# A Mamba and channel-mix layer: the start laid out anew, with channel mix's weights on GpSimd's queue and other orders of the steps

## The chip, the core and the metric

The kernel runs on one core of a Trainium2 chip. Its five engines work side by side and wait for each other by semaphores: PE (TensorE, matrix products into PSUM), DVE (VectorE), ACT (ScalarE), POOL (GpSimd) and SP, which here only issues transfers. A transfer can be issued from the queue of SP, of ACT or of POOL. The metric is the time of one execution on the device in microseconds (us); shorter is better. PSUM has eight banks of 128 x 512 f32: here two hold the sum y (y_ps), three the decays (da_ps), and three (w0_ps, w1_ps, w2_ps) are shared by all other products.

## What is computed

x is 4 x 2048 x 256, f32. Two blocks follow each other, each added to its input:

```python
# Mamba block on xn = layernorm(x)
xz = xn @ W_in;  x_, z = halves of xz;  proj = x_ @ W_x
delta = softplus(proj[..., :D] @ W_dt + b_dt);  B, C = the 2*16 other columns of proj
h = exp(delta * A[n]) * h + delta * x_ * B[n]        # along the sequence, for 16 states n
y = sum over n of h * C[n] + x_ * D_param
h1 = x + layernorm((y * silu(z)) @ W_out + xn) * ln_g + ln_b
# channel mix on hn = layernorm(h1), hp = hn of the token before
r = sigmoid((mu_r*hn + (1-mu_r)*hp) @ W_r.T)
k = relu((mu_k*hn + (1-mu_k)*hp) @ W_k.T)**2
out = h1 + r * (k @ W_v.T)
```

## The kernel before

**Tiling.** The tokens are cut into 16 chunks of 512 (4 per sequence). Step t works at once on three or four chunks: it scans chunk t, prepares chunk t+1 (the units xnT, bc, dt, x, z), finishes the Mamba block of chunk t-1 (gT, wo, xa) and does channel mix for chunk t-2 (hT, r, k, v, xo). Step -1 is the start, with the preparation of chunk 0 alone; step 15 and `close` are the end.

**A step.** The scan of a chunk has 16 columns (states n). For each, ACT makes the decays exp(delta*A) of both channel halves in da_ps (L646); POOL makes dbx = u * B (L530, up to three columns ahead of the step's own count, in a ring of four); DVE scans both halves (L1018). Times C and into hg: on DVE for the columns in `SPLITS` (L1025), on POOL for the others (L543). PE adds hg into y_ps by products with the identity (L1267). The carry of a column to the next chunk is copied by ACT (L652, L657). With three da_ps banks, ACT can be at most about one column and a half ahead of DVE.

**What sets the order.** All other work is hung between these columns by hand-written tables: `ACT_TURN` and `VEC_TURN` name a place (0 to 31, two for each column), `PE_TURN` a column (0 to 15), `BANK` one of the three shared banks. `_HEAD` and `_TAIL` tables do the same for step -1 and step 15. Each engine runs its list strictly in order, so a stage that waits holds up all that stands behind it on its engine.

**The start.** SP loads W_in, W_x, x, W_dt and then nine further things: mu_r, mu_k, ln_b, W_r, W_k, W_v, W_out, ln_g, ln_b again, all counted on one semaphore (`w_loaded`, 9 loads). PE turns W_in by transposes (`turn_weight`, L1218), multiplies W_x and then W_dt into it (L1229, L1236), and ACT copies each result out of PSUM (`folded_weight`, L620), so that delta comes from xn in one product. DVE takes the moments of x (L953), ACT its rsqrt (`first_rsqrt`), DVE the norm (L967); PE turns xn (L1301), ACT copies it to xnT. Then PE makes bc (the B and C rows), dt, x, z. bc goes through HBM and comes back spread over all partitions (b_ring, c_ring); only the first two B rows are spread on the chip, by products with `pick` (L1346) that ACT copies to b_ring (L694, `first_column`).

After these, at place 25 of its list, DVE scales channel mix's weights (`scale_ffn_weights`, L976 to L983): PE turns W_r, W_k (in the banks of the two spread rows, so it waits for both copies, `b_begun`) and then W_v (`turn_ffn_weights`, at column 12), and DVE writes six results. Then DVE takes the norm of chunk 1. All of it stands ahead of the first scan in DVE's list. One semaphore, `start_read`, counts how many of the start's units are read, in their order.

## Time and profile before

| | us |
|---|---|
| median of 3 runs | 975.38 (974.22 to 981.02) |
| the profiled execution, whole | 975.23 |
| its span on the core | 973.4 |

| engine | busy us | share of the span | instructions |
|---|---|---|---|
| PE | 897.7 | 92% | 4830 |
| DVE | 906.3 | 93% | 921 |
| ACT | 851.6 | 87% | 2060 |
| POOL | 885.5 | 91% | 392 |

The span is what lies between the first and the last instruction on the core; the time of a run is 1.8 us longer here. Every row of a timeline gives the start, how long the engine was busy, the engine, the line of the code, what was written from what, how many instructions are merged, and in brackets how long the engine had been idle and what ended that. A run of n instructions that overlap a little takes less than n times the duration of one.

### The profile page before, as it was taken

To read this page: it belongs to the slowest core of one execution; us is meant where nothing else is said; L and a number is where in the kernel's file an instruction comes from. 1 tells how busy PE (TensorE), PEld (TensorE's weight loads), DVE (VectorE), ACT (ScalarE), POOL (GpSimd) and SP (SyncE) were. 2 spreads that over 40 slices of the span, in tenths; PEclk is the share of its full clock that TensorE was granted. 3 is DMA by queue.
4 is the path that set the end of the run, shared out by engine and by line. 5 is a ranking of instruction groups with operands and counts; after the bars stand their busy time and mean duration, and the time that the engine had idled before them with its cause. 6 is when DMAs were issued, how large, how long until landed. Compare 5 with 4: busy or idle time off the path is not lost.

```text
span 973.4 us, 15457 instructions
## 1 busy us (share of the span) xinstructions
PE 897.7 (92%) x4830; PEld 695.1 (71%) x4830; DVE 906.3 (93%) x921; ACT 851.6 (87%) x2060; POOL 885.5 (91%) x392
## 2 busy tenths in 40 slices
PE   7676787999999999999999999999999999999997
PEld 4345475777877677786777688776868778788886
DVE  2799999999999999999999999999999999999765
ACT  3486888999999999998999999999999999988855
POOL 1689999999999989999999989999999998999970
PEclk9798787999999999999999999999999999999999
DMA  6426553465455626355454635556353644544320
GB/s 192 169 89 216 198 199 127 152 238 177 174 219 195 231 101 248 139 197 197 195 196 160 252 113 200 193 196 240 150 196 133 238 165 184 215 174 156 130 76 23
DMA packets 51472, 171.44 MB, mean 176 GB/s; under 512 B 5440, under 2 KB 32576, under 8 KB 35136
## 3 DMA queue, kind: packets, MB, share of 16 engines
q1 hardware_dynamic: 50576, 170.44, 47.8%
q8 instruction: 39, 0.64, 0.3%
q14 instruction: 41, 0.34, 0.1%
q10 hardware_dynamic: 816, 0.02, 0.0%
HBM read 153.15 MB, written 9.44 MB: 167 GB/s over the span
## 4 chain that ended last, share of the span: by engine, by line
PE 51%; ACT 26%; DVE 16%; issue 7%; DMA 0%; DVEq 0%; ACTq 0%
PE w_ps L1276 13%; PE w_ps L1283 10%; PE y_ps L1267 8%; ACT da_ps L646 8%; DVE da_ps L1018 6%; PE w_ps L1292 5%; PE w_ps L1295 5%; DVE hg L1018 4%; ACT h_tok L596 3%; DVE hg L1025 3%; PE w_ps L1360 3%; PE w_ps L1301 3%; ACT xres L850 2%; ACT h_tok L582 2%; ACT xn_tok L582 2%
## 5 line engine op out<-in xcount | busy, mean ns | idle before, releaser
L530 POOL TENSOR_TENSOR dbx<-u,b_ring 128x1024 f32<-128x1024 f32 x255 | 599.3, 2382 | 14.9 <-DVE da_ps L1018 6.4
L646 ACT ACTIVATE da_ps<-delta,a_neg 128x512 f32<-128x512 f32 x512 | 343.1, 685 | 17.4 <-DVE hg L1025 10.6
L543 POOL TENSOR_TENSOR hg<-hg,c_ring 128x1024 f32<-128x1024 f32 x123 | 292.5, 2378 | 18.1 <-ACT carry L652 17.9
L1267 PEld LDWEIGHTS y_ps<-ident,hg 128*128 128x128 f32 x2048 | 233.8, 143 | 43.9 <-issue 28.7
L1267 PE MATMUL y_ps<-ident,hg 128*128 128x128 f32 x2048 | 255.1, 276 | 10.3 <-POOL hg L543 10.3
L1018 DVE TENSOR_TENSOR_SCAN da_ps<-da_ps,carry,dbx 128x512 f32<-128x512 f32 x200 | 245.7, 1272 | 2.5 <-ACT da_ps L646 2.5
L1018 DVE TENSOR_TENSOR_SCAN hg<-da_ps,carry,dbx 128x512 f32<-128x512 f32 x184 | 224.9, 1267 | 5.8 <-ACT da_ps L646 5.4
L1025 DVE TENSOR_TENSOR hg<-da_ps,c_ring 128x1024 f32<-128x1024 f32 x132 | 160.9, 1219 | 8.4
L1018 DVE TENSOR_TENSOR_SCAN da_ps<-da_ps,dbx 128x512 f32<-128x512 f32 x64 | 75.5, 1215 | 1.9 <-ACT da_ps L646 1.7
L1018 DVE TENSOR_TENSOR_SCAN hg<-da_ps,dbx 128x512 f32<-128x512 f32 x64 | 75.3, 1210 | 2.1 <-ACT da_ps L646 1.9
L1276 PE MATMUL w_ps<-xnT,w_in 128*128 128x512 f32 x120 | 58.3, 631 | 4.8 <-DVE zs L1054 4.5
L1292 PE MATMUL w_ps<-w_rT,mixed 128*128 128x256 f32 x240 | 61.7, 380 | 1.0 <-DVE mixed L1062 1.0
L1295 PE MATMUL w_ps<-w_r_prev,mixed 128*128 128x256 f32 x240 | 61.6, 379 | 0.0
L1283 PE MATMUL w_ps<-w_in,xnT 128*128 128x256 f32 x248 | 59.6, 384 | 0.2 <-ACT delta L680 0.2
L1276 PE MATMUL w_ps<-mixed,w_kT 128*128 128x512 f32 x120 | 57.0, 598 | 2.6 <-DVE mixed L1062 2.6
L1283 PE MATMUL w_ps<-w_out,gated 128*128 128x256 f32 x248 | 58.6, 379 | 0.0
L1276 PE MATMUL w_ps<-xnT,w_dtx 128*128 128x512 f32 x120 | 55.0, 601 | 1.3 <-DVE mixed L1062 0.7
L1283 PE MATMUL w_ps<-w_vT,kact 128*128 128x256 f32 x240 | 54.4, 379 | 0.0
L1283 PEld LDWEIGHTS w_ps<-w_out,gated 128*128 128x128 f32 x248 | 47.1, 190 | 6.4
L1295 PEld LDWEIGHTS w_ps<-w_r_prev,mixed 128*128 128x128 f32 x240 | 45.6, 190 | 6.2
L1283 PEld LDWEIGHTS w_ps<-w_in,xnT 128*128 128x128 f32 x248 | 45.6, 193 | 5.7 <-ACT delta L680 0.5
L1292 PEld LDWEIGHTS w_ps<-w_rT,mixed 128*128 128x128 f32 x240 | 44.3, 190 | 7.0 <-DVE mixed L1062 1.2
(194 smaller groups left out, 1339.4 us busy)
## 6 DMA issues: line engine op xcount, KB each, us to landing
c_ring<-bc_rows_dram SPq DMA_DIRECT2D x64, 1024.0 KB, 4.7
b_ring<-bc_rows_dram SPq DMA_DIRECT2D x63, 1024.0 KB, 6.3
xres<-in_L_attn_x_in_dram SPq DMA_DIRECT2D x16, 512.0 KB, 4.8
x_tok<-in_L_attn_x_in_dram SPq DMA_DIRECT2D x15, 512.0 KB, 5.9
res<-xn_tok SPq DMA_DIRECT2D x15, 512.0 KB, 3.2
out_dram<-r_out SPq DMA_DIRECT2D x15, 512.0 KB, 3.2
bc_rows_dram<-bc_rows SPq DMA_DIRECT2D x16, 64.0 KB, 6.4
w_in<-in_L_attn_W_in_dram SPq DMA_DIRECT2D x2, 256.0 KB, 4.5
```

The source lines that it names most:

```text
L530: pool.tensor_tensor(dbx[:, n % X_RING, :, :], u[:, ip, :, :], b.to_broadcast([P, KH, LC]), ALU.mult).then_inc(s["dbx_done"], 1)
L543: pool.tensor_tensor(part, part, c_of(n).to_broadcast([P, KH, LC]), ALU.mult).then_inc(s["g_pool"], 1)
L582: last = act.activation(dst[j], src[j], ACT.Identity, scale=rs[j], bias=nm[j])
L596: last = act.activation(spare[:, j, :], src[:, j, :], ACT.Square, bias=nm[ln][:, j:j + 1], accum_out=sq[ln][:, j:j + 1])
L646: act.activation(da_of(n, h), delta[:, ip, h, :], ACT.Exp, scale=a_neg[:, h, n:n + 1]).then_inc(s["da_ready"], 1)
L1018: dve.tensor_tensor_scan(out, da_of(n, h), dbx[:, n % X_RING, h, :], 0.0 if first else carry[:, n, h:h + 1], ALU.mult, ALU.add).then_inc(s ...
L1025: dve.tensor_tensor(hg[:, n % H_RING, :, :], da_both(n), c_of(n).to_broadcast([P, KH, LC]), ALU.mult).then_inc(s["g_vec"], 1)
L1267: last = pe.matmul(y_tok[:, b, h * P:(h + 1) * P], hg[:, n % H_RING, h, b * P:(b + 1) * P], ident[:, :], is_transpose=True, start=n == 0 a ...
L1276: last = pe.matmul(out, w[:, k, cols], x[:, k, :], start=k == 0, stop=k == KH - 1)
L1283: last = pe.matmul(by_block(out)[:, b, :], xT_[:, k, tokens], w[:, k, :], start=b == 0 and k == 0 and not begun, stop=k == KH - 1, skip_gr ...
L1292: pe.matmul(by_block(out)[:, b, :], h_of[:, k, at_b + 1:at_b + 1 + P], w_rT[:, k, :], start=k == 0, stop=False)
L1295: last = pe.matmul(by_block(out)[:, b, :], h_of[:, k, at_b:at_b + P], w_r_prev[:, k, :], start=False, stop=k == KH - 1)
```

## The change

1. **Transfers.** W_r, W_k, mu_r, mu_k, W_v, W_out, ln_g, ln_b (twice) are issued from POOL's queue, after the identity and `pick`, and no more from SP's. `w_loaded` (now four loads) is split: `w_r_in`, `w_kv_in`, `mu_loaded` stand for the others.
2. **The start in places of its own.** `scale_ffn_weights` and `turn_ffn_weights` are cut into three, and `first_column`, `softplus`, `scale_x`, `first_rsqrt(1)`, `first_norm(1)` each get a place. On PE, W_r and W_k are turned ahead of bc, W_v after the spread rows; on ACT the moments' rsqrt comes ahead of the copy of wxT; on DVE the three scalings are spread. `start_read` becomes six semaphores, so that the units can be read in any order.
3. **Products of zeros.** DVE writes zeros to kact; PE multiplies them twice (128 x 512) ahead of everything else.
4. **Tables.** All of `ACT_`, `VEC_`, `PE_` `TURN`, `HEAD`, `TAIL`, `BANK` and `TAIL_BANK` have other numbers. The work is the same.

```diff
-ACT_HEAD = dict(xnT0=17, bc=19, xnT1=19, sp=25)
-VEC_HEAD = dict(small=5, second=7, u0=16, u1=22, ffn=25)
+ACT_HEAD = dict(xnT0=1, xnT1=3, bc=3, sp0=3, sp1=9, x1=16, rsq1=24, col0=25, x0=26, col1=30)
+VEC_HEAD = dict(ffn0=2, second=3, small=11, u1=13, ffn1=14, u0=16, norm=26, ffn2=31)
...
-            for dst, src in loads:
-                sp.dma_start(dst, src).then_inc(s["w_loaded"], 16)
...
+            pool.dma_start(raw[0], halves(W_r)).then_inc(s["w_r_in"], 16)
+            pool.dma_start(raw[1], halves(W_k)).then_inc(s["w_kv_in"], 16)
+            for dst, v in ((mur, mu_r), (muk, mu_k)):
+                pool.dma_start(dst[:, :], column(v), allow_slow_non_contiguous=True).then_inc(s["mu_loaded"], 16)
+            pool.dma_start(raw[2], halves(W_v)).then_inc(s["w_kv_in"], 16)
+            pool.dma_start(w_out[:, :, :], halves(W_out)).then_inc(s["w_loaded"], 16)
...
                         folded_weight(0, w_inT, by_half(work[0]))
-                        folded_weight(1, wxT, by_half(work[1]))
                         act.wait_ge(s["a_loaded"], 48)
...
                         first_rsqrt(0)
+                        folded_weight(1, wxT, by_half(work[1]))
...
+            dve.memset(kact[:, 0, :], 0.0).then_inc(s["warm_set"], 1)
...
+            pe.wait_ge(s["warm_set"], 1)
+            for _ in range(2):
+                pe.matmul(work[1][:, :], kact[:, 0, 0:P], kact[:, 0, :], start=True, stop=True)
...
+            def turn_ffn_weight(m):
+                if m == 0:
+                    pe.wait_ge(s["w_r_in"], 16)
+                else:
+                    pe.wait_ge(s["w_kv_in"], 32)
+                if m < 2:
+                    pe.wait_ge(s["setup_ev"], 2 + m)
+                else:
+                    pe.wait_ge(s["b_begun"], 1)
+                turn_weight(FFN_BANKS[m], raw[m]).then_inc(s["ffn_turned"], 1)
...
                 def first_column(m):
...
+                    pe.wait_ge(s["pick_set"], HEAD_COLS)
+                    need_read(pe, t, "bc")
+                    pe.wait_ge(s["setup_ev"], 4)
+                    pe.wait_ge(s["ffn_set"], m + 1)
```

**DVE's list from the first norm to the first scans, before** (`w_in<-w_in` halves W_z; `w_r_prev` to `w_vT` are the scaled weights; the second `xn_tok` is the norm of chunk 1; a scan prints as SCALAR_TENSOR_TENSOR):

```order
L962 TENSOR_SCALAR w_in<-w_in 128x2x256
L988 TENSOR_SCALAR a_neg<-gated 128x32
L953 BN_STATS gated<-x_tok 128x6 x4
L957 BN_AGGR gated<-gated 128x2 x4
L1046 TENSOR_TENSOR u<-da_ps,delta 128x512
L1046 TENSOR_TENSOR u<-y_ps,delta 128x512
L976 TENSOR_SCALAR omr<-mur 128x2
...
L983 TENSOR_SCALAR w_kT<-w_ps 128x512
L983 TENSOR_SCALAR w_vT<-w_ps 128x512
L967 TENSOR_SCALAR xn_tok<-x_tok,gated,rs 128x256 x4
L1018 SCALAR_TENSOR_TENSOR da_ps<-da_ps,dbx 128x512 x2
```

The same stretch of the change:

```order
L973 TENSOR_SCALAR w_in<-w_in 128x2x256
L987 TENSOR_SCALAR omr<-mur 128x2
...
L994 TENSOR_SCALAR w_rT<-w_ps,mur 128x256
L964 BN_STATS gated<-x_tok 128x6 x4
L968 BN_AGGR gated<-gated 128x2 x4
L1001 TENSOR_SCALAR a_neg<-gated 128x32
L1059 TENSOR_TENSOR u<-da_ps,delta 128x512
L996 TENSOR_SCALAR w_kT<-w_ps 128x512
L1059 TENSOR_TENSOR u<-y_ps,delta 128x512
L978 TENSOR_SCALAR xn_tok<-x_tok,gated,rs 128x256 x4
L996 TENSOR_SCALAR w_vT<-w_ps 128x512
L1031 SCALAR_TENSOR_TENSOR da_ps<-da_ps,dbx 128x512 x2
```

W_r's four results went ahead of the second moments, W_k's between the two u; of the scalings only W_v's is left behind the norm of chunk 1.

**PE's list at the start, before** (`w_ps<-ident,h_tok` and `<-ident,gated_tok` turn W_r, W_k and W_v; `xnT,w_bc` is bc, `xnT,w_dtx` dt, `xnT,w_in` x; `w_in,xnT` is z; `bc_rows,pick` spreads a B row; the row `w_in,ident` only keeps PE busy):

```order
L1276 MATMUL w2_ps<-xnT,w_bc 32x512 x2
L1276 MATMUL da_ps<-xnT,w_dtx 128x512 x2
L1276 MATMUL da_ps<-xnT,w_in 128x512 x2
L1346 MATMUL w1_ps<-bc_rows,pick 128x512
L1276 MATMUL da_ps<-xnT,w_dtx 128x512 x2
L1276 MATMUL y_ps<-xnT,w_in 128x512 x2
L1346 MATMUL w0_ps<-bc_rows,pick 128x512
L1218 MATMUL w0_ps<-ident,h_tok 128x128 x4
L1218 MATMUL w1_ps<-ident,h_tok 128x128 x4
L1218 MATMUL w0_ps<-ident,gated_tok 128x128 x4
L1283 MATMUL y_ps<-w_in,xnT 128x256 x4
```

and of the change:

```order
L1232 MATMUL w1_ps<-ident,h_tok 128x128 x4
L1232 MATMUL w0_ps<-ident,h_tok 128x128 x4
L1295 MATMUL w2_ps<-xnT,w_bc 32x512 x2
L1295 MATMUL da_ps<-xnT,w_dtx 128x512 x4
L1295 MATMUL da_ps<-xnT,w_in 128x512 x2
L1295 MATMUL y_ps<-xnT,w_in 128x512 x2
L1362 MATMUL w0_ps<-bc_rows,pick 128x512
L1362 MATMUL w1_ps<-bc_rows,pick 128x512
L1232 MATMUL w1_ps<-ident,gated_tok 128x128 x4
L1302 MATMUL y_ps<-w_in,xnT 128x256 x4
```

Both turns of W_r and W_k now stand ahead of bc, and both spread rows behind dt and x.

**PE's list in a middle step, before** (from column 4; `ident,gated_tok` is gT, `w_rT,mixed` and `w_r_prev,mixed` are r, `ident,hg` adds a column to y):

```order
L1283 MATMUL w0_ps<-w_in,xnT 128x256 x4
L1267 MATMUL y_ps<-ident,hg 128x128 x8
L1283 MATMUL w1_ps<-w_in,xnT 128x256 x4
L1301 MATMUL w2_ps<-ident,gated_tok 128x128 x4
L1267 MATMUL y_ps<-ident,hg 128x128 x8
L1292 MATMUL w0_ps<-w_rT,mixed 128x256 x2
...
L1301 MATMUL w1_ps<-ident,gated_tok 128x128 x4
L1267 MATMUL y_ps<-ident,hg 128x128 x8
L1276 MATMUL w1_ps<-xnT,w_in 128x512 x2
L1276 MATMUL w0_ps<-xnT,w_in 128x512 x2
```

and of the change:

```order
L1320 MATMUL w1_ps<-ident,gated_tok 128x128 x4
L1302 MATMUL w0_ps<-w_in,xnT 128x256 x4
L1302 MATMUL w2_ps<-w_in,xnT 128x256 x4
L1320 MATMUL w1_ps<-ident,gated_tok 128x128 x4
L1286 MATMUL y_ps<-ident,hg 128x128 x8
L1295 MATMUL w0_ps<-xnT,w_in 128x512 x2
L1286 MATMUL y_ps<-ident,hg 128x128 x8
L1311 MATMUL w1_ps<-w_rT,mixed 128x256 x2
...
L1286 MATMUL y_ps<-ident,hg 128x128 x8
L1295 MATMUL w0_ps<-xnT,w_in 128x512 x2
```

Both gT and the first x (`xnT,w_in`) now stand ahead of r, and u0, which DVE makes from that x, moved from place 20 to 16.

## Rows read from the trace of the kernel before

**Rows 1.** The page: its head and busy time by engine.
```profile
span 973.4 us, 15457 instructions
PE 897.7 (92%) x4830; PEld 695.1 (71%) x4830; DVE 906.3 (93%) x921; ACT 851.6 (87%) x2060; POOL 885.5 (91%) x392
```

**Rows 2.** Windows: steps 0, 8, 9 and 15, each from its first scan.
```profile
core 0: us, PE busy (x) PEld busy (x) DVE busy (x) ACT busy (x) POOL busy (x), PEclk, DMA share, GB/s
35.64:91.44 55.80, 39.93 (x174) 26.75 (x172) 52.58 (x54) 38.12 (x82) 45.50 (x20) 0.83 0.41 147
486.55:541.96 55.41, 53.91 (x302) 42.46 (x301) 53.72 (x55) 53.14 (x134) 54.35 (x24) 1.00 0.53 191
541.96:598.67 56.71, 54.44 (x302) 42.40 (x301) 56.12 (x56) 53.96 (x137) 53.53 (x24) 1.00 0.51 187
879.47:943.61 64.14, 62.82 (x373) 53.28 (x372) 52.69 (x51) 50.09 (x105) 62.20 (x28) 1.00 0.33 119
```

**Rows 3.** The same view, from POOL's first product with C that follows a wait.
```profile
57.05:205.30 148.25, 120.11 (x626) 91.79 (x625) 142.40 (x135) 126.52 (x314) 145.09 (x63) 0.87 0.50 183
```

**Rows 4.** The chain that ended last, at the start: start us, us, what.
```profile
15.25 1.90 PE w_ps L1276 x4
...
20.79 1.05 PE w_ps L1346 x2
...
28.35 1.66 DVE omr L976
...
33.59 2.12 DVE xn_tok L967 x4
```

**Rows 5.** Timeline of DVE, at the start.
```profile
8.06 0.38 DVE L957 BATCH_NORM_AGGREGATE gated<-gated 128x2 f32<-128x6 f32 x4
...
35.64 2.33 DVE L1018 TENSOR_TENSOR_SCAN da_ps<-da_ps,dbx 128x512 f32<-128x512 f32 x2
...
45.12 2.32 DVE L1001 TENSOR_SCALAR w_out<-w_out,gated 128x256 f32<-128x256 f32 x2
```

**Rows 6.** Timeline of PE, at the start.
```profile
4.50 1.09 PE L1218 MATMUL w_ps<-ident,w_in 128*128 128x128 f32 x4 [4.50 <-DMA w_in<-in_L_attn_W_in_dram]
6.33 3.78 PE L1229 MATMUL w_ps<-c_ring 128*128 128x256 f32 x8 [0.75 <-ACT c_ring L620]
10.80 1.99 PE L1236 MATMUL w_ps<-c_ring 128*128 128x256 f32 x8 [0.69 <-ACT c_ring L620]
```

**Rows 7.** Timeline of ACT, at the start.
```profile
21.88 0.60 ACT L694 ACTIVATE b_ring<-w_ps 128x512 f32<-128x512 f32 x1 [2.08 <-PE w_ps L1346]
...
27.43 1.91 ACT L646 ACTIVATE da_ps<-delta,a_neg 128x512 f32<-128x512 f32 x3
```

**Rows 8.** The page's queues: transfer, issues, KB each, us from issue to landing.
```profile
h_tok<-in_L_ffn_W_r_dram SPq DMA_DIRECT2D x1, 256.0 KB, 4.1
```

**Rows 9.** Timeline of POOL: the first products, and those around step 1.
```profile
22.56 1.27 POOL L522 TENSOR_TENSOR dbx<-u,b_ring 128x512 f32<-128x512 f32 x1 [20.07 <-ACT b_ring L694]
...
27.63 6.97 POOL L530 TENSOR_TENSOR dbx<-u,b_ring 128x1024 f32<-128x1024 f32 x3
...
44.69 2.34 POOL L543 TENSOR_TENSOR hg<-hg,c_ring 128x1024 f32<-128x1024 f32 x1 [0.62 <-ACT carry L652]
...
94.77 4.69 POOL L530 TENSOR_TENSOR dbx<-u,b_ring 128x1024 f32<-128x1024 f32 x2
```

**Rows 10.** Timeline of DVE: third column of step 1, then the waits of step 8.
```profile
97.49 2.44 DVE L1018 TENSOR_TENSOR_SCAN da_ps<-da_ps,carry,dbx 128x512 f32<-128x512 f32 x2
...
522.00 0.69 DVE L1046 TENSOR_TENSOR u<-w_ps,delta 128x512 f32<-128x512 f32 x1 [0.31 <-PE w_ps L1276]
...
524.06 1.23 DVE L1018 TENSOR_TENSOR_SCAN da_ps<-da_ps,dbx 128x512 f32<-128x512 f32 x1 [0.23 <-ACT da_ps L646]
...
539.64 1.22 DVE L1018 TENSOR_TENSOR_SCAN hg<-da_ps,dbx 128x512 f32<-128x512 f32 x1 [0.53 <-ACT da_ps L646]
```

**Rows 11.** Timeline of PE in step 8: the last products of r.
```profile
517.76 1.03 PE L1295 MATMUL w_ps<-w_r_prev,mixed 128*128 128x256 f32 x4
```

More of the change, by code:

```diff
@@ L303, in need_bank @@
             if at_start(t):
-                need(eng, s["start_read"], max([use_of(t, unit) - len(START_BANKS)] + [use_of(t, v) for v in after]))
+                turn = HEAD_UNITS.index(unit)
+                before = [HEAD_UNITS[turn - len(START_BANKS)]] if turn >= len(START_BANKS) else []
+                for v in before + list(after):
+                    need_read(eng, t, v)
             else:
@@ L412, in _ @@
             sp.dma_start(w_in[:, :, D:], halves(W_in)[:, :, D:]).then_inc(s["w_z_loaded"], 16)
-            loads = [(raw[0], halves(W_r)), (raw[1], halves(W_k)), (raw[2], halves(W_v)), (w_out[:, :, :], halves(W_out))]
-            loads += [(dst[:, :], v.rearrange("(o d) -> o d", o=1).partition_broadcast(P))
-                      for dst, v in ((g_all, ln_g), (b_all, ln_b))]
-            for dst, v in ((mur, mu_r), (muk, mu_k), (b_col, ln_b)):
-                sp.dma_start(dst[:, :], column(v), allow_slow_non_contiguous=True).then_inc(s["w_loaded"], 16)
-            for dst, src in loads:
-                sp.dma_start(dst, src).then_inc(s["w_loaded"], 16)
             def slot_before(i, g):
@@ L1087, in step @@
                         first_moments(1)
-                    if start and at("ffn"):
-                        scale_ffn_weights()
+                    for m in range(3):
+                        if start and at(f"ffn{m}"):
+                            scale_ffn_weight(m)
+                    if start and at("norm"):
                         first_norm(1)
@@ L1426, in step @@
                                           is_transpose=True, start=False, stop=False, skip_group_check=True)
-                    if start and n == turn["ffn"]:
-                        turn_ffn_weights()
+                    for m in range(3):
+                        if start and n == turn[f"ffn{m}"]:
+                            turn_ffn_weight(m)
+                    for m in range(2):
+                        if start and n == turn[f"col{m}"]:
+                            first_column(m)
                     behind = column_at(t, par, n - Y_LAG, scan, pre, mid)
```

143 lines of the change are left out of this document (68 added, 75 removed).

## The prediction

> **What bounds the kernel now.** I read the page first: over the whole span four engines are busy 87% to 93% of the time [rows 1], so no share says which one sets the pace. Cutting the span at the first scan of each step does. In a middle step DVE is busy 53.72 of 55.41 us or 56.12 of 56.71 [rows 2]: its idle time is 1.7 us in step 8 and 0.6 in step 9, and part of the 0.6 is the short turn between a scan and the product that reads it. PE, ACT and POOL have 1 to 3 us left in the same steps. So DVE sets the middle steps, the others are close behind, and an order that is better can give back about 1 us in a step like 8, of which there are three (4, 8 and 12, whose sequence starts anew), and next to nothing elsewhere.
>
> The two ends differ. DVE's first scan starts at 35.64 [rows 5]. In step 0 DVE is idle for only 3.2 of 55.8 us; POOL is idle for 10.3 there [rows 2], but from 57.05 to 205.30 it works 145.09 of 148.25 us [rows 3]. In that stretch it is at least as tight as DVE: the product for the third column of step 1 is the first of the two that run from 94.77 for 4.69 us, so it is over at about 97.1 [rows 9], and the scan that reads it starts at 97.49 [rows 10]. So in steps 0 to 2 a faster DVE alone would soon wait for POOL, and only a shift that takes POOL along comes through. In step 15 PE is busy 62.82 of 64.14 us [rows 2]: the end hangs on PE, whose work does not change.
>
> The start is where the time lies. In the chain that ended last, bc's product starts at 15.25 and the spread row ends at 21.84 (20.79 + 1.05); then the scalings of channel mix's weights start at 28.35 and the norm of chunk 1 at 33.59, which lasts 2.12 us [rows 4]. From 28.35 to the scan at 35.64, 7.3 us, DVE does nothing that the first scan needs, while decays are there from 27.43 on [rows 7] and POOL has its ring full at 34.60 (27.63 + 6.97) [rows 9].
>
> **The change, part by part.** I lay the new start out with these durations.
>
> *Zeros, and the chain to bc.* Today PE is idle until W_in lands, and turns it at 4.50. The eight products with W_x take 3.78 us, while eight of the same form take 1.99 us from 10.80 on [rows 6]: TensorE is at the lower of its two clocks (1.2 GHz) before and at the upper (2.4) after. The zeros are two 128 x 512 products; four rows of that form, two products, take 1.90 us at the upper clock [rows 4], so some 3.8 at the lower. PE is free from about 1.5 us, so they end at about 5.2: the turn of W_in starts 0.7 later. If the clock rises by the time of the W_x products, these give back up to 3.78 - 1.99 = 1.8. Bounds: +0.7 (no earlier rise) to -1.1. But ACT now takes the rsqrt of x's moments ahead of the copy of wxT. The moments are done at 8.44 [rows 5] if x lands as now, and W_r and W_k will share the transfers of x and W_dt; I allow them 0.5 us. That leaves a gain of 0.9 of the 1.1. Then PE turns W_r and W_k ahead of bc: four transposes take 1.09 at the lower clock [rows 6], so two turns take 1.1 at the upper, of which some 0.7 lie in the gap in which PE waits for xnT anyway. bc starts at 15.25 - 0.9 + 0.4 = 14.75.
>
> *From bc to the first scan.* Three units (bc, dt, x) fill 15.25 to 20.79, 1.85 each [rows 4]. Now five stand ahead of the spread rows: 14.75 + 9.2 = 23.95. Two spread rows at 1.05: 26.0. ACT's copy 0.6 [rows 7], its copy of x 0.6 more, and the first decay a third of 1.91, 0.65 [rows 7]: 27.9. Meanwhile DVE has u1, W_k's scaling, u0 and the norm of chunk 1 (no more behind POOL's products, see below) done by about 26; W_v is turned after the first copy (26.6 + 0.55) and scaled by about 27.8. **First scan at 27.9 instead of 35.64: 7.8 us.** POOL's first product moves the other way, from 22.56 [rows 9] to 26.6, and it then has no wait for u. Can POOL take that up? From 22.56 to step 1 at 91.44 are 68.9 us, of which it is idle for 2.6 (23.83 to 26.4, between the two halves of its first column [rows 9]) and 10.3 [rows 2]: 56.0 of work. In the change it has from 26.6 to 91.44 - 7.8 = 83.6, that is 57.0. It fits by 1.0. So I let the 7.8 through, and count nothing more for steps 0 to 2.
>
> *DVE against POOL.* In the trace, 128x2 work of DVE that starts at 28.35 takes 1.66 us and ends at 30.01 [rows 4], as the first of POOL's three ends (27.63 + about 2.33); the first of W_out's two results at 45.12 ends only with POOL's product of 44.69 + 2.34, together 2.32 us [rows 5, 9]. DVE and POOL shut each other out there. In the change POOL works through at W_out's place, so both results may wait: I take 0.3 lost; bounds: 1 gained (a free gap) to 2.3 lost. The norm of chunk 1, today at 33.59, lies ahead of POOL's first product in the change.
>
> *POOL's queue.* No row shows a transfer issued there. From SP's queue W_r takes 4.1 us to land [rows 8]. PE wants W_r at about 13.7 and W_k with W_v at about 14.2; W_v is the fifth issue after 2.5 us. PE holds nothing up if an issue costs POOL up to (14.2 - 4.1 - 2.5) / 5 = 1.5 us. The bounds are nothing and 2.3 us, POOL's longest usual instruction, which would cost 0.8 x 5 = 4 us, for PE waits ahead of bc with everything behind it. I take no loss.
>
> A rule of the Trainium skill speaks against this part (SBUF — State Buffer, Who interferes with whom): the lock between DVE and GpSimd that the rows above show also stops GpSimd from writing the descriptors of transfers that it issues itself, while DVE is in a 2-port mode. DVE's norm and its halving of W_z are five results of 0.4 us in that stretch, so by that page the estimate is up to 2 us later for W_v, and a sum of 968.5 if the issues alone use up the margin. No row shows it either way.
>
> *Tables in the middle.* In step 8 DVE waits 0.31 for x from PE, 0.23 and 0.53 for ACT [rows 10]. The first x now stands ahead of r, 7 us earlier, and u0 four places earlier: the first wait goes. r ends later: 518.79 (517.76 + 1.03) now [rows 11]; the order puts x and gT1 ahead of it and an added column behind, net some 1.8 us, which comes close to when ACT wants it (place 19). Moving hT ahead of xnT on ACT delays bc by about 1.1 us, which PE takes up as hT is done in that gap. I take DVE's 0.31 and 0.23 as gone in the three steps like 8, and for r's lateness 0.07 a step in the nine others: 3 x -0.54 + 9 x 0.07 = -1.0. Bounds: -3.3 (all avoidable idle time of steps 4, 8 and 12) and +1 a step, the size of the largest of these shifts. In the tail, -1.3 (PE's idle time in step 15) to +3; taken: -0.2.
>
> **Sum**: -7.8 + 0.3 - 1.0 - 0.2 = -8.7. Against the profiled execution, 975.23, that gives 966.5; the median of the runs is 975.38, the same.
>
> **The rivals.** (a) *The weights come late.* PE stands before W_r, W_k and W_v with bc behind them. For: three semaphores and a queue that the trace never shows. Against: 7.6 us for five issues. Price by the bound 4: 970.5; it decides from 1.5 us an issue on. (b) *The gain is spent in POOL or given back.* POOL has 1.0 to spare until step 1; it decides from there on, and if 4 us go (a shut-out at W_out of 2.3, a carry that comes late), DVE waits for products in step 1: 966.5 + 3 = 969.5. (c) *The new middle order is slower.* r comes 1.8 us later to an ACT that then still has a table load and two decays ahead of DVE; if PE runs late, ACT stands at place 19 and DVE with it, in every step. It decides from 0.65 us a step (13 steps make up for 8.7); at 1.1 us a step the time is 975.2 - 7.7 + 14.3 = 981.8, slower than before. For: ACT has only 2 to 3 us idle in a step. Against: PE loses two waits of its own. (d) *More than forecast*: the clock stays up through the start, W_out's results fall in a gap, steps 0 to 2 lose part of the waits behind a slow PE: 961.5. (e) *Nothing comes of it*: the first scan is early but its C rows, which come through HBM, are not there. bc's copy is about 0.6 earlier than now, and the second half scan ends at 30.3; I see no more than 0.3 us in it.
>
> **Chances.** Forecast (964 to 969) 0.56; (a) and (b) together 0.20; (c) 0.11, of which 0.06 end above 985; (d) 0.13. Range 961 to 976. A measurement tells about 1% from no change, that is 965.6 and 985.1. Faster than 965.6: (d) 0.13 and half of the forecast 0.28: 0.41. Slower 0.05. Within: 0.54.
>
> **What would show it.** Right: the first scan at 27 to 29; no DVE work on weights between u0 and it but W_v's; POOL's first product at 26 to 27 and hardly idle until 50; POOL idle in step 0 near 1 to 3 us; DVE's idle time in steps 4, 8 and 12 under 1.3. Wrong: PE waiting for h_tok's or gated_tok's transfer before bc; DVE idle for dbx in step 1; ACT waiting for r at the tanh of each step; middle steps longer than 56.2 on average.

## The result, and the profile after the change

The changed kernel takes 966.98 us (median of 6 runs, 966.0 to 967.84) against 975.39 for the kernel before (6 runs, 974.22 to 981.02): the ratio is 0.9907, with a 95% interval of 0.9884 to 0.993. That is within 1% by the bound of the prediction, and the interval shows that it is a gain. The profiled execution took 967.01, its span is 965.1.

The page has the same picture as before [rows 1]: the span is shorter by 8.3 us, every engine's share of it is a point higher, and PE and DVE work a little less (by 3.9 and 1.9 us). Only POOL works clearly more, by 6.8 us: its nine issues of transfers are counted as busy, and loads_on_sp below, where SP makes them, shows 885.5 again.

```profile
span 965.1 us, 15450 instructions
...
PE 893.8 (93%) x4834; PEld 697.5 (72%) x4834; DVE 904.4 (94%) x922; ACT 852.8 (88%) x2060; POOL 892.3 (92%) x401
```

The windows of steps 0, 8, 9 and 15, each from its first scan, answer to [rows 2]. The columns are the stretch, its length, each engine's busy time (and instructions), the granted clock, the DMA share and GB/s.

```profile
27.27:83.83 56.56, 39.07 (x176) 26.86 (x175) 53.41 (x52) 39.72 (x85) 54.01 (x24) 0.85 0.44 166
479.30:534.64 55.34, 53.51 (x302) 42.55 (x301) 53.68 (x55) 53.09 (x134) 55.34 (x25) 1.00 0.52 192
534.64:591.59 56.95, 54.50 (x302) 42.58 (x301) 56.23 (x55) 54.21 (x138) 54.20 (x24) 1.00 0.50 186
871.92:935.66 63.74, 61.86 (x365) 52.49 (x364) 52.51 (x51) 50.52 (x105) 61.30 (x27) 1.00 0.34 120
```

The first scan starts 8.37 us earlier (27.27 for 35.64). Step 0 is 0.76 longer than before and POOL's idle time in it is down from 10.3 to 2.55. Step 8 is 0.07 shorter, step 9 is 0.24 longer, and steps 3 to 14 together are 0.12 shorter: the new order of the middle steps is worth nothing to speak of.

Timeline of DVE at the start (start, length, engine, line, operation, tiles, count, idle before and what ended it), to be read beside [rows 5]:

```profile
13.87 0.48 DVE L993 TENSOR_SCALAR w_r_prev<-w_ps,omr 128x256 f32<-128x256 f32 x1 [2.38 <-PE w_ps L1232]
...
17.17 0.15 DVE L1001 TENSOR_SCALAR a_neg<-gated 128x32 f32<-128x32 f32 x1
21.48 0.69 DVE L1059 TENSOR_TENSOR u<-da_ps,delta 128x512 f32<-128x512 f32 x1 [4.16 <-PE da_ps L1295]
22.08 0.68 DVE L996 TENSOR_SCALAR w_kT<-w_ps 128x512 f32<-128x512 f32 x1
23.19 0.69 DVE L1059 TENSOR_TENSOR u<-y_ps,delta 128x512 f32<-128x512 f32 x1 [0.43 <-PE y_ps L1295]
23.80 1.37 DVE L978 TENSOR_SCALAR xn_tok<-x_tok,gated,rs 128x256 f32<-128x256 f32 x4
26.44 0.69 DVE L996 TENSOR_SCALAR w_vT<-w_ps 128x512 f32<-128x512 f32 x1 [1.26 <-PE w_ps L1232]
27.27 2.35 DVE L1031 TENSOR_TENSOR_SCAN da_ps<-da_ps,dbx 128x512 f32<-128x512 f32 x2
```

W_r's four scalings stand at 13.87, W_k's at 22.08, the norm of chunk 1 at 23.80; only W_v's 0.69 us is left between them and the scan. And DVE has 4.16 us free before u1, which nothing fills yet. The timeline of PE, beside [rows 6], has the zeros, and both groups of eight products at the upper clock:

```profile
1.56 3.76 PE L1238 MATMUL w_ps<-kact 128*128 128x512 f32 x4 [1.56 <-POOL ident L503]
5.11 1.06 PE L1232 MATMUL w_ps<-ident,w_in 128*128 128x128 f32 x4
6.92 1.99 PE L1246 MATMUL w_ps<-c_ring 128*128 128x256 f32 x8 [0.75 <-ACT c_ring L632]
9.60 1.99 PE L1253 MATMUL w_ps<-c_ring 128*128 128x256 f32 x8 [0.69 <-ACT c_ring L632]
11.43 0.97 PE L1259 MATMUL w_ps<-c_ring 128*128 128x32 f32 x8
12.24 1.07 PE L1320 MATMUL y_ps<-ident,xn_tok 128*128 128x128 f32 x8
13.15 1.04 PE L1232 MATMUL w_ps<-ident,h_tok 128*128 128x128 f32 x8
14.12 1.90 PE L1295 MATMUL w_ps<-xnT,w_bc 128*32 128x512 f32 x4
```

What came back in step 0 is in two rows at W_out's centring, DVE's and POOL's, that answer to 45.12 and 44.69 in [rows 5, 9]:

```profile
36.77 3.17 DVE L1014 TENSOR_SCALAR w_out<-w_out,gated 128x256 f32<-128x256 f32 x2
```

```profile
30.48 9.32 POOL L541 TENSOR_TENSOR dbx<-u,b_ring 128x1024 f32<-128x1024 f32 x4
39.76 2.39 POOL L554 TENSOR_TENSOR hg<-hg,c_ring 128x1024 f32<-128x1024 f32 x1
```

The two results take 3.17 us where they took 2.32. One by one, the first ends at 37.60 and the second at 39.95, each 0.15 us behind the end of a product of POOL (37.45 and 30.48 + 9.32 = 39.80). Before, only the first waited like this.

### The profile page after: what moved, and what is told of

It is laid out like the page before. It is cut to its first block, busy times and chain, and to the rows that moved or that the text cites. A ratio compares the mean times of both kernels' runs of the same rounds, so it can differ in the third digit from the quotient of the medians.

```text
span 965.1 us, 15450 instructions
## 1 busy us (share of the span) xinstructions
PE 893.8 (93%) x4834; PEld 697.5 (72%) x4834; DVE 904.4 (94%) x922; ACT 852.8 (88%) x2060; POOL 892.3 (92%) x401
## 4 chain that ended last, share of the span: by engine, by line
PE 32%; DVE 30%; ACT 27%; issue 9%; DMA 1%; DVEq 0%; SPq 0%; ACTq 0%
DVE da_ps L1031 13%; ACT da_ps L654 9%; PE w_ps L1295 9%; DVE hg L1031 8%; DVE hg L1038 7%; PE w_ps L1302 6%; PE y_ps L1286 5%; ACT xn_tok L593 3%; PE w_ps L1311 3%; PE w_ps L1314 3%; ACT h_tok L607 2%; PE w_ps L1320 2%; ACT xres L860 1%; PE w_ps L1376 1%; PE da_ps L1295 1%
## 5 line engine op out<-in xcount | busy, mean ns | idle before, releaser
L654 ACT ACTIVATE da_ps<-delta,a_neg 128x512 f32<-128x512 f32 x512 | 338.1, 682 | 21.4 <-DVE hg L1038 8.5
L1286 PEld LDWEIGHTS y_ps<-ident,hg 128*128 128x128 f32 x2048 | 237.8, 144 | 44.0 <-issue 29.9
L1286 PE MATMUL y_ps<-ident,hg 128*128 128x128 f32 x2048 | 259.0, 277 | 11.4 <-POOL hg L554 8.4
L1295 PE MATMUL w_ps<-xnT,w_dtx 128*128 128x512 f32 x120 | 57.6, 605 | 0.0
```

The source lines that it names most:

```text
L654: act.activation(da_of(n, h), delta[:, ip, h, :], ACT.Exp, scale=a_neg[:, h, n:n + 1]).then_inc(s["da_ready"], 1)
L1286: last = pe.matmul(y_tok[:, b, h * P:(h + 1) * P], hg[:, n % H_RING, h, b * P:(b + 1) * P], ident[:, :], is_transpose=True, start=n == 0 a ...
L1295: last = pe.matmul(out, w[:, k, cols], x[:, k, :], start=k == 0, stop=k == KH - 1)
```

## The experiments

Twelve kernels, in four groups; those of a group ran on one chip, beside the kernel before. The table has what their profiles show: when the upper clock first sets in by the trace's record of TensorE's clock, the first scan, POOL's first product, the lengths of steps 0, 1 and 2, what follows from the first scan of step 3 to the end, and then the median of all runs and the ratio to the kernel before with its interval. The ratio lies near that of the means, so it can differ from that of the medians, as in tables_only.

| kernel | clock up | first scan | POOL | step 0, 1, 2 | rest | median | ratio |
|---|---|---|---|---|---|---|---|
| before | 10.63 | 35.64 | 22.56 | 55.80, 56.28, 57.59 | 768.12 | 975.39 | 1 |
| changed | 6.83 | 27.27 | 25.72 | 56.56, 57.08, 56.97 | 767.25 | 966.98 | 0.9907 (0.9884 to 0.993) |
| head_only | 6.73 | 27.26 | 25.71 | 56.47, 56.58, 57.62 | 767.54 | 967.35 | 0.99 (0.9882 to 0.9919) |
| tables_only | 14.47 | 37.38 | 24.30 | 56.88, 57.35, 57.70 | 767.50 | 977.42 | 0.9999 (0.998 to 1.0018) |
| centre_early | 10.55 | 29.24 | 27.50 | 55.89, 58.09, 58.23 | 767.43 | 967.13 | 0.9904 (0.9884 to 0.9923) |
| more_before_scan | 5.88 | 28.76 | 25.64 | 57.05, 57.35, 57.02 | 767.07 | 969.53 | 0.9926 (0.9908 to 0.9944) |
| no_zeros | 14.55 | 30.34 | 28.78 | 57.17, 57.15, 57.81 | 766.83 | 970.30 | 0.9928 (0.9903 to 0.9953) |
| loads_on_sp | 5.79 | 27.14 | 25.58 | 56.13, 55.52, 58.06 | 767.52 | 966.84 | 0.9906 (0.9883 to 0.993) |
| centre_fill | 4.37 | 27.33 | 25.77 | 52.75, 58.16, 55.77 | 767.24 | 965.15 | 0.9885 (0.986 to 0.991) |
| centre_fill_table | 6.43 | 27.27 | 25.72 | 51.88, 59.88, 58.26 | 767.25 | 965.19 | 0.9884 (0.9862 to 0.9905) |
| hold_clock | 6.87 | 27.27 | 25.72 | 56.65, 56.11, 55.77 | 767.24 | 966.21 | 0.9904 (0.9879 to 0.9928) |
| centre_fill_hold | 10.74 | 29.07 | 27.51 | 52.29, 58.69, 55.77 | 767.25 | 964.94 | 0.9883 (0.9861 to 0.9905) |
| centre_fill_table_hold | 4.66 | 26.99 | 25.44 | 51.93, 59.23, 55.77 | 767.27 | 964.69 | 0.9882 (0.986 to 0.9903) |
| one_column_less | 5.96 | 27.32 | 25.77 | 52.22, 57.37, 55.77 | 766.89 | 960.49 | 0.9843 (0.9814 to 0.9871) |

### Start or tables?

`head_only` is the changed kernel with the middle and tail tables (ACT_TURN to BANK, ACT_TAIL to TAIL_BANK) of before; `tables_only` is the kernel before with those of the change. The order of the start's units, which BANK's order decides on ties, stays in each as it was.

> The new start with the tables of before for the middle steps and the tail. The change took 8.4 us off the median; the first scan came 8.4 us earlier (35.64 to 27.27 in the profiles). Theory A, the start is all of it: the first scan stays at 27.3 and the median is within 0.6 us of the changed kernel's 967.0, that is 966.5 to 967.6. Theory B, my prediction's sizes hold: the new tables are worth 1.2 us, so this kernel takes 968.2. Theory C, the tables hide a loss (steps 0 and 1 gave back 1.6 us because of them): this kernel takes 965.5 or less. In the profile the waits of DVE in step 8 should be those of before again (0.31, 0.23, 0.53).

> The start of before with the new tables for the middle steps and the tail. Theory A: 975.4 to within 0.6 us, and the step starts of before. Theory B: 974.2, with steps 4, 8 and 12 shorter by 0.5 us each. Theory C: 977 or more, with steps 0 to 1 longer by 1.6 us.

head_only takes 967.35, which is theory A, and its step 8 has the waits of before again (0.31, 0.23 and 0.52). For tables_only the outcome is mixed. Its median, 977.42, and its steps 0 and 1, 2.15 us longer, are what theory C named; its mean, 976.86 against 976.82 for the kernel before, and the ratio of 0.9999 are theory A, with an interval of 1.8 us either way. So the start is all of the gain as far as these runs can tell, and no more than 1.8 us of the tables, either way, could have been missed. From step 3 on the profiled run of the changed kernel is 0.3 us shorter than head_only's, that of tables_only 0.6 shorter than the kernel before's. Of DVE's waits in step 8 the changed kernel has these:

```profile
501.29 1.23 DVE L1031 TENSOR_TENSOR_SCAN da_ps<-da_ps,dbx 128x512 f32<-128x512 f32 x1 [0.60 <-ACT da_ps L654]
516.96 1.23 DVE L1031 TENSOR_TENSOR_SCAN da_ps<-da_ps,dbx 128x512 f32<-128x512 f32 x1 [0.23 <-ACT da_ps L654]
521.24 1.23 DVE L1031 TENSOR_TENSOR_SCAN da_ps<-da_ps,dbx 128x512 f32<-128x512 f32 x1 [0.20 <-ACT da_ps L654]
```

The waits of 0.31 for x and of 0.53 for ACT are gone [rows 10], 0.23 stands as before, and 0.60 and 0.20 for ACT are new: 1.03 us together, where there were 1.07. The spread of tables_only (single runs 973.45 to 979.9) and its profile's late first scan led to the next question: in its profile the upper clock sets in 3.84 us later than in the one of before.

### The zeros

```diff
-            dve.memset(kact[:, 0, :], 0.0).then_inc(s["warm_set"], 1)
...
-            pe.wait_ge(s["warm_set"], 1)
-            for _ in range(2):
-                pe.matmul(work[1][:, :], kact[:, 0, 0:P], kact[:, 0, :], start=True, stop=True)
```

> The changed kernel without the two products of zeros. In the profiles that have them the clock rose at 6.83, 6.73, 5.88 and once at 10.55 (centre_early); in the two that do not, at 10.63 and 14.47. Theory A, the zeros bring the rise forward by one step of that kind: without them W_x's eight products take 3.8 us instead of 1.99 in most runs, the turn of W_in starts 0.6 earlier (4.5), and the sum is 1.2 us later at the first scan (28.5) and at the end: 968.2. Theory B, when the clock rises does not depend on the zeros: 966.4, 0.6 us less than the changed kernel. Theory C, later rises are common without them (as at 14.47, which cost 1.7 us more in tables_only): 969 or more, with a wide spread.

970.3, with single runs in two groups (966.9 twice; 969.5 to 971.8 four times): theory C. The profile fell into the second group. Timeline of PE of no_zeros:

```profile
4.56 1.08 PE L1231 MATMUL w_ps<-ident,w_in 128*128 128x128 f32 x4 [4.56 <-DMA w_in<-in_L_attn_W_in_dram]
6.39 3.78 PE L1242 MATMUL w_ps<-c_ring 128*128 128x256 f32 x8 [0.75 <-ACT c_ring L632]
10.86 3.78 PE L1249 MATMUL w_ps<-c_ring 128*128 128x256 f32 x8 [0.69 <-ACT c_ring L632]
```

W_x's and W_dt's eight products both take 3.78 us; in the changed kernel both take 1.99, and in the kernel before the first eight took 3.78 and the second 1.99 [rows 6]. So the start knows three cases, and the zeros make the first likely: of the eleven profiles with zeros nine have the upper clock from 4.4 to 6.9 us on and two from about 10.6; of the three without, one has it at 10.63 and two at about 14.5. As far as the rise PE runs the same list in all eleven (the zeros from 1.56 on for 3.4 to 3.8 us, then W_in's turn, and in the two late ones W_x's products too), and the same in the three (idle until about 4.5, W_in's turn, W_x's products). What picks the case within each group is not shown. By medians the zeros are worth 3.3 us, by the ratios 2.0 with overlapping intervals, by the lowest times (966.0 and 966.88) 0.9. No profile shows where the clock rose in the two fast runs of no_zeros.

This also divides the gain at the first scan. With the rise at 14.5 it comes at 37.38 in the old order and at 30.34 in the new one: 7.04 us. With the rise at 10.6 it is 35.64 and 29.24 (centre_early, whose centring lies in idle time): 6.40. The remaining 1.97, down to 27.27, goes with the clock: W_x's eight products take 3.77 us in centre_early and 1.99 in the changed kernel, which is 1.78 of it.

### POOL's queue

```diff
-            pool.dma_start(raw[0], halves(W_r)).then_inc(s["w_r_in"], 16)
+            sp.dma_start(raw[0], halves(W_r)).then_inc(s["w_r_in"], 16)
...
```

> The changed kernel with the nine loads of channel mix's weights issued by SP behind its seven others, in the same order, instead of by POOL. In the kernel before, SP's W_r landed at 10.02, W_k at 10.75 and W_v at 11.52; from POOL's queue they landed at 8.82, 9.76 and 11.58, and PE turned the first at 13.15. Theory A, the queue is worth nothing because both are there in time: first scan at 27.3, 967.0 to within 0.6. Theory B, it matters through W_z, which landed at 10.89 instead of 9.30 with POOL's loads beside it, and made DVE wait 0.45 us: up to 0.4 less, 966.6. Theory C, PE waits for a weight from SP: 967.5 or more.

966.84: theory A, the queue is worth nothing. In the changed kernel PE takes up W_r at 13.15 without a wait, and POOL's idle time lies there anyway. The transfers themselves are no faster from POOL's queue. The page's queues of the changed kernel (transfer, issues, KB, us from issue to landing), and of loads_on_sp:

```profile
h_tok<-in_L_ffn_W_r_dram POOLq DMA_DIRECT2D x1, 256.0 KB, 6.2
...
h_tok<-in_L_ffn_W_k_dram POOLq DMA_DIRECT2D x1, 256.0 KB, 6.3
gated_tok<-in_L_ffn_W_v_dram POOLq DMA_DIRECT2D x1, 256.0 KB, 5.9
```

```profile
h_tok<-in_L_ffn_W_r_dram SPq DMA_DIRECT2D x1, 256.0 KB, 5.1
h_tok<-in_L_ffn_W_k_dram SPq DMA_DIRECT2D x1, 256.0 KB, 5.5
gated_tok<-in_L_ffn_W_v_dram SPq DMA_DIRECT2D x1, 256.0 KB, 4.8
```

### DVE against POOL, and what bounds step 0

```diff
                     if start and at("small"):
                         small_constants()
+                        center_w_out()
...
                             silu(-1, m, par)
-                        center_w_out()
```

> The changed kernel with W_out's centring taken out of step 0 and put into the start, right behind the scaling of the exponentials at 17.3, where DVE is idle for 4.2 us and POOL has no product yet. In the changed kernel's profile the centring takes DVE from 35.71 to 39.87, 4.16 us, of which its last two results are 3.17 us for what took 2.32 in the kernel before. Theory A, DVE and POOL shut each other out there: without POOL's products beside it the centring takes some 1.8 us, all of it in the idle time, the two last results under 1 us together; the third column's scan comes 4.1 us earlier. Theory B, the two results are slow by themselves: they take 3.2 us (or 2.3) in the start as well, and delay u1. For the whole time: POOL has no idle time from 50 to 134 us and 2.55 in step 0, and its product for the third column of step 1 is 1.1 us ahead of its scan. If POOL is the bound of steps 0 and 1, at most 2.55 + 1.1 = 3.6 come through: 963.4 to 964.5. If DVE alone is the bound, 4.1: 962.8. If something else (ACT's exponentials) holds steps 0 to 2, under 2: above 965.

For the centring itself this came out as theory A. In the start the two results take 0.62 us, in DVE's idle time and with POOL idle. Timeline of DVE of centre_early:

```profile
20.07 0.62 DVE L1014 TENSOR_SCALAR w_out<-w_out,gated 128x256 f32<-128x256 f32 x2
23.25 0.69 DVE L1059 TENSOR_TENSOR u<-da_ps,delta 128x512 f32<-128x512 f32 x1 [2.57 <-PE da_ps L1295]
```

So they are not slow by themselves: 0.62 with POOL idle, 2.32 with one gap of POOL's, 3.17 in the changed kernel. In more_before_scan, where they start at another point of POOL's row of products, they take 3.92. Timelines of DVE, then POOL, of more_before_scan:

```profile
38.26 3.92 DVE L1018 TENSOR_SCALAR w_out<-w_out,gated 128x256 f32<-128x256 f32 x2
```

```profile
28.10 11.58 POOL L541 TENSOR_TENSOR dbx<-u,b_ring 128x1024 f32<-128x1024 f32 x5
39.63 2.40 POOL L554 TENSOR_TENSOR hg<-hg,c_ring 128x1024 f32<-128x1024 f32 x1
```

POOL's instructions end at 39.68 and 42.03, DVE's two results at 39.82 and 42.17. Each of DVE's two waits for the end of the instruction of POOL that is under way. The Trainium skill says (SBUF — State Buffer, Who interferes with whom) that, when DVE is in a 2-port mode, whichever of DVE and GpSimd issues first holds the shared ports for the whole instruction and the other is blocked fully; the rows agree.

The third column's scan then came 3.9 us nearer to the first. Yet the median is 967.13, no gain, which is the case that the expectation left to something else than POOL or DVE. (The profile is of the slowest run, 970.75, with the late clock.) The fourth column's second scan waits. Timelines of centre_early, DVE, then PE:

```profile
41.55 1.21 DVE L1031 TENSOR_TENSOR_SCAN hg<-da_ps,dbx 128x512 f32<-128x512 f32 x1
45.88 2.34 DVE L1031 TENSOR_TENSOR_SCAN hg<-da_ps,dbx 128x512 f32<-128x512 f32 x2 [3.11 <-ACT da_ps L654]
```

```profile
38.41 5.09 PE L1326 MATMUL w_ps<-w_in,ident 128*128 128x512 f32 x8 [5.10 <-DVE zs L1067]
43.33 1.04 PE L1320 MATMUL w_ps<-ident,xn_tok 128*128 128x128 f32 x8
```

PE's four filler products (eight rows) stand behind its wait for DVE's zs and ahead of the turns of chunk 1's norm; ACT waits for those turns (5.24 us at its xnT) with the decays queued behind. In the changed kernel the same chain ran beside DVE's centring and was only just hidden. Its timelines, PE, then ACT:

```profile
36.15 6.06 PE L1326 MATMUL w_ps<-w_in,ident 128*128 128x512 f32 x8 [6.29 <-DVE zs L1067]
```

```profile
43.87 1.30 ACT L654 ACTIVATE da_ps<-delta,a_neg 128x512 f32<-128x512 f32 x2
```

The first of the two decays ends at about 44.5, and its scan starts at about 44.6, with no wait to be seen. Step 0 of centre_early is still 0.7 us shorter; its fillers took less time too (5.09 for 6.06), which may be the reason. The next kernel is centre_early with the fillers taken out of the chain:

```diff
                 if t == 0:
+                    pe.wait_ge(s["b_begun"], HEAD_COLS)
+                    keep_busy(work[0], 4)
                     need_all_read(pe, -1, HEAD_UNITS)
                     pe.wait_ge(s["ffn_set"], 3)
-                    keep_busy(work[0], 4)
```

> centre_early with one thing more: PE's four filler products (128x512) at the head of step 0 stand ahead of its wait for z to be read, and no longer between that wait and the turns of chunk 1's norm. In centre_early the third column's scan came 3.9 us earlier against the first (8.73 behind it instead of 12.60), but the fourth waited 3.11 us for ACT's decays at 45.88, ACT for the turns on PE (5.24 us), and PE started the fillers only at 38.41, behind DVE's zs. Theory A, that chain (zs, fillers of 5 to 6 us, turns, xnT, decays) is the second bound of step 0: now that wait is gone, the fifth column's scan is 3 us nearer to the first scan than in centre_early, and the median is 3 us lower than centre_early's 967.1: 964.0. Theory B, POOL lets no more than its idle time through: 965 or more. Theory C, the wait comes from elsewhere: 967.

Step 0 falls to 52.75 us: the chain is the second bound of step 0, as theory A says. This does not hang on the clock, for centre_fill_hold below has the late rise, as centre_early has, and a step 0 of 52.29. But the median, 965.15, is theory B's and not A's 964.0: POOL has no idle time in step 0 any more, and step 1 grows to 58.16. Timelines of centre_fill, DVE, then PE:

```profile
97.94 1.28 DVE L1031 TENSOR_TENSOR_SCAN hg<-da_ps,carry,dbx 128x512 f32<-128x512 f32 x1 [2.59 <-ACT da_ps L654]
```

```profile
92.65 3.62 PE L1295 MATMUL w_ps<-xnT,w_bc 128*32 128x512 f32 x4
96.20 3.84 PE L1295 MATMUL w_ps<-xnT,w_dtx 128*128 128x512 f32 x8
```

bc's four products take 3.62 us, at the lower clock, and ACT waits for them with the decays behind it. The kernels with zeros in steps 0 and 1, below, show that this wait is not what held step 1.

Another kernel also moves ACT's table load for the tanh of z into ACT's idle time before it:

```diff
+                    if t == 0 and place == 0:
+                        act.preload_act_table_set(EXP_TANH)
                     if t == 0 and place == 2:
-                        act.preload_act_table_set(EXP_TANH)
```

> centre_fill with ACT's table load for the tanh of z moved from ahead of the tanh into ACT's idle time of 2.1 to 2.3 us before it. DVE waits 1.32 us for zs there. If DVE and not POOL sets step 0: 1.2 us less than centre_fill, 962.8. If POOL is the bound by then (it has no idle time from 50 us to 134 us): the same as centre_fill.

965.19, the same as centre_fill: DVE's wait of 1.32 for zs is gone, step 0 is 0.87 shorter, and step 1 takes back more than that (59.88 for 58.16). Whether by POOL or by the clock, this kernel can't say.

### Does a delay ahead of the first scan reach the end?

```diff
+                if m == 2:
+                    for dst in (r_out[:, 0:2, :], r_out[:, 2:4, :]):
+                        dve.tensor_scalar(dst, turned, 0.5, None, ALU.mult)
+                    last = dve.tensor_scalar(kact[:, 1, :].rearrange("p (k n) -> p k n", k=KH), turned, 0.5, None, ALU.mult)
                 last.then_inc(s["ffn_set"], 1)
```

> The changed kernel with three more scalings of W_v by DVE (into r_out and kact, which nothing needs yet) right behind its own, ahead of the first scan: about 1.9 us more of DVE's work, with POOL's first product where it was. If what comes ahead of the first scan reaches the end one for one: first scan at 29.2 and 968.9. If POOL sets the pace from 50 us on (it has no idle time there), the delay is taken up by its idle time of 2.55 us in step 0 and by DVE's waits: under 1 us more, 967.9 or less. If the three are stretched by POOL's products beside them (each 0.69 us alone), the first scan comes later than 29.5.

969.53, 2.55 more than the changed kernel: what comes ahead of the first scan reaches the end. The first scan comes 1.49 later and 0.74 more is lost at W_out's centring (3.92 for 3.17); at the end of the scans 2.10 is left. So nothing of it is absorbed: in the changed kernel DVE and not POOL sets steps 0 to 2, and POOL's idle time in step 0 only grows, to 4.65.

### The clock in steps 0 and 1, and POOL as the last bound

```diff
                     if behind:
                         add_up(behind[0], behind[2])
+                        if behind[0] in (0, 1) and behind[2] < NS - 1:
+                            for _ in range(1):
+                                pe.matmul(y_ps[:, 0, :], kact[:, 0, 0:P], kact[:, 0, :], start=False, stop=False,
+                                          skip_group_check=True)
```

kact is zero until step 2, so y's sum stays what it is.

> The changed kernel with one product of zeros (128x512) added to y's sum behind each column of steps 0 and 1 but the last, while PE waits for the next column. In all profiles so far the granted clock is at the upper level from about 155 us on without a break, but in steps 0 to 2, where PE is idle for 11 to 17 us a step, it falls to half of it six to eight times, at other places in each run; bc's four products of step 1 took 1.93 us in the changed kernel and 3.62 in centre_fill, where DVE then waited 2.59 for the decays behind them. Theory A, this falling clock is what steps 0 to 2 lose and what makes the times spread: the clock stays up in steps 0 and 1, DVE's waits there fall below 2 us a step, steps 0 to 2 take 169 instead of 170.6, and the median is 965.3 with a smaller spread. Theory B, the clock there costs nothing on the path: 967.0, or more, as the added products (0.95 us each) delay what PE does behind them.

> centre_fill with the same products of zeros. Theory A: step 1 keeps what centre_fill won in step 0 (3.8 us, of which the wait of 2.59 at 97.94 took 2.6 back in the profile): step 1 takes 55.8 instead of 58.16 and the median is 963, against 965.15. Theory B: no difference from centre_fill, 965.2. Theory C, POOL, which has no idle time in steps 0 and 1 there, now holds DVE: waits of DVE for dbx in step 1, over 1 us together.

> centre_fill_table with the same products of zeros. In its profile DVE first waited for POOL (0.39 and 0.77 us for dbx in step 1), having come 5.3 us ahead of the changed kernel. If the clock alone took its gain back: 1.2 us less than centre_fill_hold. If POOL is the bound from there on: the same as centre_fill_hold to within 0.4.

In hold_clock steps 1 and 2 take 111.88 us instead of 114.05, and step 3 starts 2.07 earlier (195.81 for 197.88). Steps 0 to 2 take 168.53 us, as theory A says, where the changed kernel took 170.61; but loads_on_sp, whose start has other queues and whose steps are the same, took 169.71 without zeros. The median is only 0.8 lower, between the two theories and with overlapping runs, so the gain stands in the profile and not in the times. In centre_fill_hold the wait of 2.59 is gone, but step 1 is no shorter (58.69), and step 2 starts at 140.04 as in hold_clock, though step 0 was 4.4 us shorter. The windows from POOL's first product to step 2's first scan say why. Columns as above; of the changed kernel, of hold_clock, of centre_fill, of centre_fill_hold, of centre_fill_table_hold:

```profile
25.72:140.91 115.19, 85.73 (x419) 63.81 (x420) 108.21 (x103) 87.70 (x208) 112.64 (x50) 0.85 0.48 179
```

```profile
25.72:140.04 114.32, 95.56 (x441) 61.88 (x442) 108.10 (x104) 87.73 (x208) 111.75 (x50) 0.96 0.48 179
```

```profile
25.80:138.24 112.44, 87.19 (x414) 62.66 (x415) 103.96 (x98) 87.99 (x208) 111.61 (x50) 0.83 0.49 183
```

```profile
27.30:140.04 112.74, 96.41 (x440) 63.41 (x441) 104.18 (x97) 87.74 (x209) 112.53 (x50) 0.95 0.50 182
```

```profile
25.40:138.15 112.75, 96.29 (x440) 62.98 (x441) 104.39 (x97) 87.50 (x208) 112.71 (x50) 0.95 0.49 181
```

In the last two POOL is busy for all but 0.2 us, and the stretch is 112.7 us in both, whenever it begins. The zeros lift the granted clock from 0.83 or 0.85 to 0.95 or 0.96. Yet centre_fill took no longer for the stretch at 0.83, 112.4 us with POOL busy for all but 0.8: so the clock is not what held it there. (centre_fill_table took 113.31, with POOL busy throughout: the length of POOL's own work varies by a us or two.) In centre_fill_table_hold DVE waits for POOL:

```profile
76.61 2.34 DVE L1032 TENSOR_TENSOR_SCAN hg<-da_ps,dbx 128x512 f32<-128x512 f32 x2 [0.76 <-POOL dbx L541]
85.85 2.47 DVE L1032 TENSOR_TENSOR_SCAN da_ps<-da_ps,carry,dbx 128x512 f32<-128x512 f32 x2 [0.77 <-POOL dbx L541]
```

That is the second case of centre_fill_table_hold, 964.69. For centre_fill_hold, 964.94, the median is theory B's. The sign of theory C did not come, as DVE waits for dbx only once in step 1, for 0.45 us and not for over 1; that POOL holds the stretch there rests on its busy time alone. The last kernel takes work from POOL:

```diff
-            return LAST_SPLIT if i == LAST else SPLITS[i % 2]
+            return LAST_SPLIT if i == LAST else SPLITS[1 if i == 0 else i % 2]
```

> centre_fill_table_hold with one change: in step 0 the product of state and C of column 3 is made by DVE (1.2 us) and no longer by POOL (2.35 us), as it is already in the odd steps. In centre_fill_hold and centre_fill_table_hold POOL is busy for 112.5 of 112.7 us between its first product and the first scan of step 2, whenever the first product starts (27.51 and 25.44), so POOL's work sets steps 0 and 1. Theory A: with 2.35 us less of it, the stretch from POOL's first product to step 2 becomes shorter by 2.0 to 2.35, that is 110.4 to 110.7, and the median is 2 us lower than 964.7: 962.6. Theory B, DVE or ACT holds it as closely: under 0.8 us less, 964.

Step 2 starts 111.15 us behind POOL's first product (136.92 - 25.77), 1.6 less. That is less than theory A's 2.0 to 2.35 and more than theory B's 0.8. POOL is busy for 111.01 of them: with one product of 2.35 us less, its other 49 took 0.65 us more. The median is 960.49, 4.2 less than 964.69, measured on another chip. The profiled run itself took 961.42, 1.6 less than that of centre_fill_table_hold, which fits the stretch; the rest of the median's 4.2 has no place in the profiles and is left open (the five runs are 960.22 to 963.23). So theory A holds in direction; its size is 1.6 in the profiles and open in the times. This kernel beats the kernel before and the changed one: 0.9843, with an interval of 0.9814 to 0.9871. Against centre_fill_table_hold the intervals overlap a little.

## Why the prediction held, step by step

The forecast was 966.5, in a range of 961 to 976; it came out at 966.98. By the profiles the sum is -8.37 at the first scan, +0.94 in steps 0 to 2, -0.12 in steps 3 to 14, -0.40 in step 15 and -0.34 behind it: -8.29, where -7.8, +0.3, -1.0 and -0.2 were forecast (-8.7). The mechanism of the start, which makes up the gain, was right; the closeness of the sum is in part luck, for several terms were off and cancelled.

- **The start, -7.8.** Measured -8.37. From bc to the first scan the layout by hand gave 13.15 us (14.75 to 27.9), and 13.15 is what it took (14.12 to 27.27). That it is the same to the last digit is luck: the five units took 8.90 us for 9.2, and from the end of the spread rows to the scan there were 2.27 for 1.9. bc itself came 0.63 earlier than laid out, which is the whole difference to -7.8. Two allowances were not needed: 0.2 for ACT's rsqrt (the gap between W_x's and W_dt's products is 0.69 before and after) and 0.4 for the two turns (bc follows them with a wait of 0.17, for ACT's xnT). Ahead of bc the step "the eight products give back up to 1.8" was right in the profile, but it took the case without zeros from one execution, in which W_dt's products were fast. no_zeros shows that these can be slow too: the term was 3.3 us by medians and 2.0 by the ratios, not 1.1, and the sum named no chance of the late cases.
- **POOL takes up the shift; it fits by 1.0.** Right, though the sum was wrong: it left out that POOL is also idle from 34.60, with its ring full, to 35.64. The work until step 1 was 54.95 us and not 56.0, so that by its own rows it fits by 2.0. Measured are 115.19 us with 112.64 of work until step 2, 2.5 to spare, all of it in step 0. more_before_scan and hold_clock show DVE as the bound there, the three kernels behind them that POOL is next, and how far off.
- **W_out, +0.3.** The mechanism was right, the size was not: 0.85 more, within the bounds of -1 to 2.3. "Both results may wait" with POOL working through means that each waits for the end of a product, and where in a product DVE arrives sets the price (3.17, or 3.92). With products of 2.33 us back to back that could have been counted; the estimate is 2.3 to 4.6 us for the two.
- **POOL's queue, nothing.** Right: W_r landed at 8.82, W_k at 9.76 and W_v at 11.58, PE wanted the first at 13.15; an issue costs POOL 0.88 the first time and 0.55 to 0.73 from then on, half of the 1.5 at which it would have decided. But a transfer took 6 us to land where the sum had 4.1, so the margin for W_v, which PE waited for together with W_k at about 13.7, was 2.1 us. W_z is later (10.89 for 9.30), which cost DVE 0.45 us in idle time. The rule of the Trainium skill that DVE's 2-port modes stop GpSimd from writing descriptors (SBUF — State Buffer, Who interferes with whom) was not put to the test: POOL's last issue was over at 8.9 and DVE's norm began at 9.08. Its estimate of 2 us later for W_v did not come about.
- **The middle tables, -1.0.** This step failed. The median of head_only puts them at 0.4 us, the two profiles' rest at 0.3, and the interval of tables_only holds no change. The sign that the prediction named, DVE idle for under 1.3 us in steps like 8, did not come: it is 1.66 in step 8, where it was 1.69. The wait for x went, as forecast, but 0.23 did not, and "I take them as gone" left out that ACT's decays are then in other places too: 0.60 and 0.20 us of waiting for them took the place of 0.31 and 0.53. Which move brought the 0.60 was not tried. Step 9 is 0.24 longer, not 0.07.
- **Nothing more in steps 0 to 2.** The prediction read PE's falling clock there (0.83 in [rows 2]) and gave it no price. hold_clock puts it at 1.2 to 2.1 us by profiles, 0.8 by medians. It was there before and after (0.83 and 0.85 in step 0), so it will have left the difference alone; whether it makes the spread of the times was not shown.
- **The rivals.** (a), weights late, is out by the rows above. (b), a gain spent in POOL, did not occur at this size of gain; its mechanism is what the last four kernels ran into. (c) is out by head_only. (d), more than forecast, had half of its condition: the clock was up from 6.83 to 34.13, but W_out's results fell in no gap, and steps 0 to 2 became longer. (e), C rows late, did not show.
